# Reading a value tile back in two pieces, in a fused whitening, attention and expert kernel

## The reference

```
x = iter_norm_whiten(x)                       # statistics over all positions, 16 channels a group
t = to_tokens(x)                              # 16 x 3136 x 64
t = t + LN(local_attention(LN(t)))            # each token sees itself and 16 neighbours to each side
t = t + moe(LN(t))                            # 8 experts, the best 2 per token, gelu
# local_attention:
kv_pad = pad(x, ((0, 0), (16, 16), (0, 0)))
windows = kv_pad[:, arange(N)[:, None] + arange(33)[None, :]]
scores = einsum('bnd,bnwd->bnw', x, windows) / 8
out = einsum('bnw,bnwd->bnd', softmax(scores), windows)
```

## Time and profile before

| | |
|---|---|
| median of 3 runs | 1121.23 us (1112.76 to 1134.49) |
| the profiled execution | 1112.64 us |
| its span | 1110.9 us |
| PE / DVE / ACT busy | 94% / 81% / 51% |
| mean granted TensorE clock | 0.96 |
| DMA, SP's queue (q1) | 96.91 MB, 35.1% of 16 engines |

### The profile page before, as it was taken

One profiled execution on the slowest core, in us unless ns is written; L12 is line 12 of the kernel. 1 busy time (PEld: TensorE's weight loads), 2 busy tenths in 40 slices (PEclk: granted clock), 3 DMA queues, 4 the chain that ended last, 5 costly groups with the idle time before them and its releaser, 6 DMA issues.

```text
span 1110.9 us, 26094 instructions
## 1 busy us (share of the span) xinstructions
PE 1048.4 (94%) x9158; PEld 692.8 (62%) x9158; DVE 904.3 (81%) x2575; ACT 565.4 (51%) x917; POOL 148.3 (13%) x179
## 2 busy tenths in 40 slices
PE   7947999999999999998799999999999999999998
PEld 7935777777777777776455555555555555555553
DVE  6944888887888887887788888888888888888785
ACT  0014655655566555653455555555555555555553
POOL 7021232232223222231000000000000000000000
PEclk9959999998999999995799999999999999999999
DMA  9604555554555555543122222222222222222221
GB/s 290 238 9 105 142 131 147 136 133 113 143 138 136 142 135 137 136 120 90 42 67 70 71 66 67 71 70 66 74 66 67 68 73 66 70 71 66 67 71 44
DMA packets 244750, 111.51 MB, mean 100 GB/s; under 512 B 199392, under 2 KB 242656, under 8 KB 243888
## 3 DMA queue, kind: packets, MB, share of 16 engines
q1 hardware_dynamic: 235456, 96.91, 35.1%
q10 hardware_dynamic: 8064, 12.85, 3.4%
q0 software_dynamic: 1136, 0.56, 0.2%
HBM read 71.60 MB, written 38.67 MB: 99 GB/s over the span
## 4 chain that ended last, share of the span: by engine, by line
PE 82%; ACT 9%; DVE 4%; issue 3%; DMA 2%; SPq 0%; POOL 0%; DVEq 0%; ACTq 0%; POOLq 0%
PE p L1138 17%; PE p L1113 16%; PE p L1123 10%; PE p L1087 7%; PE p L971 7%; ACT prob L569 5%; PE p L1060 4%; PE p L964 4%; PE p L981 4%; ACT xt_s L521 3%; PE p L1082 3%; DMA resid<-in_x_dram 2%; PE p L1134 2%; PE p L979 2%; PE p L1008 2%
## 5 line engine op out<-in xcount | busy, mean ns | idle before, releaser
L586 ACT ACTIVATE arena<-p,b_s 128x896 f32<-128x896 f32 x224 | 225.5, 1007 | 231.0 <-PE p L1113 229.6
L890 DVE TENSOR_TENSOR arena<-arena,p 128x896 f32<-128x896 f32 x224 | 242.5, 1083 | 76.4 <-PE p L1123 74.8
L1138 PE MATMUL p<-arena,w_s 128*64 128x448 f32 x896 | 215.2, 559 | 0.3 <-DVE arena L890 0.3
L1113 PE MATMUL p<-thl,w_hi 128*128 128x448 f32 x448 | 165.2, 450 | 0.4 <-DVE thl L862 0.4
L1113 PE MATMUL p<-thl,w_lo 128*128 128x448 f32 x448 | 127.3, 365 | 0.0
L1123 PE MATMUL p<-arena,selector 128*128 128x448 bf16 x448 | 123.9, 358 | 1.8 <-DVE arena L890 1.4
L1123 PEld LDWEIGHTS p<-arena,selector 128*128 128x128 bf16 x448 | 25.4, 97 | 159.0 <-issue 116.9
L1113 PEld LDWEIGHTS p<-thl,w_hi 128*128 128x128 f32 x448 | 85.6, 192 | 21.2 <-issue 0.6
L479 POOL TENSOR_TENSOR yb<-yb,bet 128x448 f32<-128x448 f32 x56 | 59.2, 1058 | 253.5 <-DVE xn_s L828 253.5
L569 ACT ACTIVATE prob<-p 96x896 f32<-96x896 f32 x56 | 51.1, 912 | 78.2 <-PE p L1087 78.2
L1113 PEld LDWEIGHTS p<-thl,w_lo 128*128 128x128 f32 x448 | 84.9, 189 | 7.6
(11 more groups left out here) (177 smaller groups left out, 1640.6 us busy)
## 6 DMA issues: line engine op xcount, KB each, us to landing
tn_spill<-tnt_s ACTq DMA_DIRECT2D x56, 224.0 KB, 2.7
arena<-tn_spill SPq DMA_DIRECT2D x56, 224.0 KB, 3.4
t_s<-tn_spill SPq DMA_DIRECT2D x56, 224.0 KB, 2.5
arena<-in_x_dram SPq DMA_DIRECT2D x112, 96.0 KB, 2.6
xn_rows<-xn_s SPq DMA_DIRECT2D x56, 192.0 KB, 2.1
out_dram<-arena SPq DMA_DIRECT2D x112, 96.0 KB, 1.8
resid<-in_x_dram SPq DMA_DIRECT2D x6, 1568.0 KB, 14.2
v_a<-xn_rows SPq DMA_DIRECT2D x56, 168.0 KB, 3.3
```

The costliest lines, as they stand in the source:

```text
L586: a.activation(hid[:, j % 2, :].rearrange("p (h n) -> p h n", h=H), (p34 if j % 2 == 0 else p56)[:, :, 0:CH], ACT.Gelu, bias=b1_s[:, j:j + ...
L890: v.tensor_tensor(gated[:, j % 2, :].rearrange("p (h n) -> p h n", h=H), hid[:, j % 2, :].rearrange("p (h n) -> p h n", h=H), p01[:, :, 0: ...
L1113: last = t.matmul(bank[:, h, 0:CH], w[:, 128 * j:128 * (j + 1)], thl[:, c, h, :], start=(k == 0), stop=(k == 1))
L1138: last = t.matmul(p2[64 * h:64 * h + 64, 0:CH], w2_s[:, j, :], gated[:, j % 2, h * CH:(h + 1) * CH], start=False, stop=(j == 3))
```

## The change

The seven blocks of a value tile are read in two pieces. Six of them (blocks 0 to 5) need only rows up to the end of the chunk itself: they are read in iteration g for chunk g, as soon as `rows_out(g)` has landed and PV of chunk g-2, which used the same tile, is over. The last block is read in the next iteration, behind the rows of the next chunk. A value tile is now filled by four DMAs instead of two, and PV waits for 64 counts instead of 32. The bytes are the same.

```
-        def windows(n, at_q, h):
+        def windows(n, at_q, h, blocks):
...
-                           [[H * C, KEYS], [BLK * H * C, NB], [1, C]])
+                           [[H * C, KEYS], [BLK * H * C, blocks], [1, C]])
...
-            def values_in(q):
-
-                at_q = q % CPI * CH
-                sp.wait_ge(s_xw, 48 * min(q + 2, G))
-                wait(sp, s_o, q - 1)
+            def values_in(q, blocks):
+
+                at_q = q % CPI * CH + blocks[0] * BLK
+                tile = values[q % 2][:, blocks[0]:blocks[-1] + 1]
                 for h in range(H):
-                    sp.dma_start(values[q % 2][:, :, h, 0:C], windows(q // CPI, at_q, h)).then_inc(s_vd[q % 2], 16)
+                    sp.dma_start(tile[:, :, h, 0:C], windows(q // CPI, at_q, h, len(blocks))).then_inc(s_vd[q % 2], 16)
...
                 if g < G:
                     rows_out(g)
+                sp.wait_ge(s_xw, 48 * min(g + 1, G))
                 if g > 0:
-                    values_in(g - 1)
+                    values_in(g - 1, [NB - 1])
+                if g < G:
+                    wait(sp, s_o, g - 1)
+                    values_in(g, range(NB - 1))
...
-                    pe.wait_ge(s_vd[q % 2], 32 * (q // 2 + 1))
+                    pe.wait_ge(s_vd[q % 2], 64 * (q // 2 + 1))
```

## The result

The changed kernel takes **1162.75 us** (median of 4 runs, 1150.22 to 1177.92) against 1117.49 us (1112.76 to 1134.49) for the kernel before. The ratio, of the fast executions alone, is 1.038, with a 95% interval of 1.025 to 1.051: slower. The profiled execution took 1150.22 us, with a span of 1148.3.

A forecast was written before the change was run, and what follows sets the result against it. PE was taken to bound the kernel by under a microsecond a step, SP next. To the profiled 1112.6 us, SP's longer steps added 25.5 (1138) and five clock falls 17.5, giving 1156 us, range 1116 to 1182.

The forecast's parts named there:

- SP becomes the bound: In the pipeline, SP's demand rises from 6.98 to 8.2 us a step, above PE's 7.42 and the present 7.69.
- The price of the two issues: On SP's queue, two more DMAs a chunk cost 0.9 to 1.15 us a step, taken as 1.1.
- The landing of the last block: On SP's path to PV, the second read of the last block lands in 2.2 us, between 1.8 and 2.4.
- The room of 2.1 us: Between xn_s and PV, SP may once fall 2.1 us behind without harm: 7.9 us available, 5.8 needed.
- The clock: PE standing ahead of PV loses its granted clock: five falls at 3.5 us net each, 17.5 us in all.
- The early reads' wait for PV: On SP, the six-block reads wait for PV of chunk g-2: costed at 0, up to 0.3 us a step otherwise.
- Idle time ahead of PV: In the profile after, PE's idle time ahead of PV grows from 9 to about 40 us, on "issue".
- The waits of before: PE's waits ahead of PV for the value tile: their removal is worth at most 9.1 us, at least 0.
- The fast rival: In the pipeline, the block lands earlier, SP keeps up and all PV waits go: 1103.5 us, chance 0.08.

The follow-up runs named there:

- the filled run: The changed kernel with three more bias matmuls in every whitening, whose result is overwritten: 1147.07 us.
- the old order on a free SP: The kernel before, whole tiles read behind the next chunk's rows, with all token loads issued by GpSimd, 5 DMAs a step left on SP: 1147.80 us.

## Why the prediction was right

**SP becomes the bound**: right, and shown. Its demand was put at 8.2 us a step. In the profile after, a step takes 8.34 us, and less SP's waits for `xn_s` (10.4 us in 48 steps, 0.22) 8.12 are left; in the filled run it is 8.37. With 9, 10 and 11 issues at the old place the demand, worked out in the same way, is 7.0, 7.6 and 8.0 us (steps of 7.69, 8.46 and 8.89 less SP's waits for other engines), and the time 1114, 1144 and 1179 us; with 9 in the new order it is 1099. The number of issues is not all: with 5 at the old place, and the loads on GpSimd, it was 1148, by the length of the path.

**The price of the two issues** was taken as 1.10 us, between 0.90 and 1.15. Measured it is 0.9: four reads in 1.84 us against two in 0.90 to 0.94.

**The landing of the last block**, 2.2 us (1.8 to 2.4) in the sum, is 1.8. The room of 2.1 us was about right: with the stores 2.1 to 2.7 us behind `xn_s`, PE waited 0.1 to 0.4 us ahead of the PV that needs them in five steps, and 1.33 in a sixth, where 4.9 us went by from the first store to the first read instead of 3.6 to 4.0. But SP does not stay at that point, it falls 3.1 to 3.9 us behind around each fall of the clock, and can win back that much. This made the next term smaller.

**The clock**: five falls taken, five seen in the profiled execution. One was priced at 3.5 us net. SP's waits for `xn_s` are what a fall still costs after SP has caught up, 10.4 us for five, 2.1 each. That is the mis-sized term: 17.5 us in the sum, 10.4 measured. The sum for the 52 steps was 25.5 + 17.5 = 43 us; measured are 34.0 in the fastest of the four executions. The demand of 8.12 instead of 8.22 is the other 5 us, and the 2.1 us of room, taken off in the sum, go the other way. The median is 12.5 us higher than this one; the mean granted clock is lower in the other three executions (0.904 to 0.916 against 0.932), so they have more time at half clock, but only this one has a trace, and how their falls lie was not seen. The predicted 1156 lies between, and that is in part luck: it is 6 us over the execution that it was worked out for, by a fall priced too high, and 7 under the median, which holds more half clock than the sum had.

**The early reads' wait for PV**, costed at 0: right, no row of it in the changed kernel. **Idle time ahead of PV**, forecast to grow from 9 to about 40 us, came to 16.7 + 14.0 = 30.7, counted in the same way.

**The waits of before**, "9.1 us at most" as the worth of the faster landing: right as a bound on what the waits alone cost (the 13.9 us above 52 x 7.42 less the 5.6 of the fall are 8.3), too small as the loss. When the waits go, the falls behind them go too: against the runs of before beside them, 1119.71 becomes 1104.21 and 1112.87 becomes 1098.51. The fast rival's 1103.5 was the right time for a kernel whose SP has room, at the wrong price of an issue.

**"It was SP's lack of room that made PE wait before"** was not said in so many words, but the expectation for the old order on a free SP rested on it. It fell: with SP 3 us freer a step PE's waits ahead of PV did not go, they grew from 3.3 to 12.1 us, and already before the change the longest had the stores on time. Why the loads on GpSimd's queue go with tiles that land 0.3 to 0.5 us later was not tested.

## What to carry to other kernels

Add up a queue's issues, landings and waits for one step before splitting a transfer on it: here the queue had 0.7 us of room in 7.4 and a DMA took 0.4 to 0.57 whatever its size, so two small reads cost 45 us and, with two other DMAs moved away, the same order gains 14 or more. A wait of PE has two prices, its own length and the clock that may fall behind it; the time at half clock in the trace gives the second. A few worthless matmuls in the place of the wait show whether it can be had back, but they lengthen the step and so shorten the wait as well. Room on the queue is not enough if the path behind it, from the store to the last landing, is as long as the time up to its use. Idle time of an engine just ahead of its step on the critical path is no free place for issues: they must also end before what it waits for arrives.

## What the runs showed of the hardware

More work made a kernel faster: 0.58 us a step of added matmuls took 15 us off the old order with the loads on GpSimd, and 16 us off the median of the changed kernel, where the ranges overlap, with the granted clock of 100 to 500 us going from 0.92 and 0.91 to 1.00. In the changed kernel a fall for 13.7 us came behind a wait of 0.54 us, while others of 1.0 to 1.3 us had none. Long issues on SP, 1.1 to 1.4 us over the usual, stand beside 16 KB packets of an instruction queue: in the changed kernel, from 100 to 500 us, 31 of the 32 single issues over 1 us have a packet within 0.5 us, and the queue has 38 packets in all. Which engine they serve, the runs don't tell.
